# First attention of a fused attention and local-transformer kernel: two buffers for scores and probabilities, a new order of its steps, and the first weight rounding on GpSimd

## What is computed

```python
x = L0_attn_X
xn = _layernorm(x, axis=-1)
x = x + _L0_attn_ref(xn, ...) + _L0_ffn_ref(xn, ...)

def _L0_attn_ref(X, W_q, W_k, W_v, b_q, b_k, b_v):      # one head of width 128
    Q = X @ W_q + b_q; K = X @ W_k + b_k; V = X @ W_v + b_v
    A = softmax(einsum('bsd,btd->bst', Q, K) * scale, axis=2)
    return einsum('bst,btv->bsv', A, V)

def _L0_ffn_ref(x, ...):
    for i in range(6):      # 16 heads of 64, windows of 32 tokens
        x = attn_layer(shift_tokens(x), Wqkv[i], ...) + x
        x = ffn_layer(shift_tokens(x), ...) + x
```

## Time and profile before

| | |
|---|---|
| device time, median of 3 runs | 1501.88 us |
| profiled execution, first to last instruction | 1500.0 us |
| first attention, TensorE's first instruction to the last add | 10.11 to 50.91 us |
| first instruction of the main part on TensorE | 51.27 us |
| TensorE busy, VectorE busy, ScalarE busy, GpSimd busy | 98%, 87%, 85%, 83% |
| mean granted TensorE clock | 0.995 |

### The profile page before, as it was taken

The page is one execution under the profiler, slowest core; times in us unless marked ns, Lnnn a source line. Parts: engine busy times, 40 slices in busy tenths (PEclk is TensorE's granted clock), DMA queues, the critical chain, the costliest instruction groups (busy, mean ns, idle before and its releaser), DMA issues.

```text
span 1500.0 us, 66306 instructions
## 1 busy us (share of the span) xinstructions
PE 1464.2 (98%) x26320; PEld 1280.8 (85%) x26320; DVE 1310.1 (87%) x2365; ACT 1267.7 (85%) x2551; POOL 1248.7 (83%) x1213
## 2 busy tenths in 40 slices
PE   6799999999999999999999999999999999999997
PEld 5578888888888888888888888888888888888886
DVE  6799998889889898888898898889898988998974
ACT  4578888889888888888898888888888888888886
POOL 5489988888888888888888888888888888888781
PEclk9899999999999999999999999999999999999999
DMA  6012212111212111121211121211112121112111
GB/s 185 22 46 60 59 46 57 43 49 42 59 49 79 52 47 43 54 63 52 70 41 50 43 70 49 69 45 50 47 40 55 52 54 38 49 35 52 38 49 39
DMA packets 96184, 80.28 MB, mean 54 GB/s; under 512 B 66282, under 2 KB 79598, under 8 KB 95854
## 3 DMA queue, kind: packets, MB, share of 16 engines
q1 hardware_dynamic: 94990, 75.34, 18.8%
q10 hardware_dynamic: 864, 0.26, 0.1%
HBM read 17.91 MB, written 1.05 MB: 13 GB/s over the span
## 4 chain that ended last, share of the span: by engine, by line
PE 93%; issue 2%; DVE 2%; POOL 1%; ACT 1%; DMA 0%; ACTq 0%; DVEq 0%; POOLq 0%
PE bank L1065 74%; PE bank L1179 11%; PE bank L1217 6%; PE bank L1251 1%; PE bank L1149 1%; DMA rot<-in_b_v 0%; POOL rot L459 0%; DVE parts L891 0%; DVE newton L910 0%; DVE s L937 0%; DVE n L901 0%; DVE am L825 0%; POOL w_lo L446 0%; ACTq L550 0%; ACT rot L576 0%
## 5 line engine op out<-in xcount | busy, mean ns | idle before, releaser
L459 POOL TENSOR_TENSOR rot<-parts 128x512 f32<-128x512 f32 x384 | 493.3, 1285 | 120.4 <-DVE parts L891 120.3
L891 DVE TENSOR_TENSOR parts<-bank,rtab 128x1024 f32<-128x1024 f32 x384 | 459.8, 1208 | 0.4 <-POOL rot L459 0.3
L470 POOL TENSOR_TENSOR rot<-rot,rnorm 128x512 f32<-128x512 f32 x384 | 391.1, 1046 | 10.0 <-DVE rnorm L917 10.0
L901 DVE TENSOR_REDUCE n<-sq 128x8 f32<-128x512 f32 x384 | 257.7, 671 | 33.0 <-ACT sq L627 33.0
L689 ACT ACTIVATE pz<-bank 64x512 f32<-64x512 f32 x384 | 226.1, 589 | 61.4 <-PE bank L1217 59.1
L1065 PE MATMUL bank<-w_hi,x_hi 128*128 128x512 f32 x576 | 263.8, 458 | 4.6 <-DVE parts L891 3.6
L476 POOL TENSOR_TENSOR es<-es,r 128x512 f32<-128x512 f32 x192 | 202.6, 1055 | 75.2 <-DVE r L943 75.2
L627 ACT ACTIVATE sq<-bank 128x512 f32<-128x512 f32 x384 | 230.4, 601 | 28.0 <-DVE n L901 22.0
L1065 PE MATMUL bank<-w_hi,x_lo 128*128 128x512 f32 x576 | 229.5, 398 | 0.0
L1065 PE MATMUL bank<-w_lo,x_hi 128*128 128x512 f32 x576 | 229.1, 398 | 0.0
L1179 PE MATMUL bank<-ident,rot 128*128 128x128 f32 x1536 | 203.1, 275 | 5.0 <-POOL rot L470 2.4
(11 more groups left out here) (86 smaller groups left out, 2660.4 us busy)
## 6 DMA issues: line engine op xcount, KB each, us to landing
vb<-v SPq DMA_DIRECT2D x96, 384.0 KB, 3.8
w_new<-in_Wqkv SPq DMA_DIRECT2D x36, 256.0 KB, 4.2
vb<-v SPq DMA_DIRECT2D x48, 128.0 KB, 3.4
w_o<-in_Wo SPq DMA_DIRECT2D x12, 256.0 KB
xin<-x_tok SPq DMA_DIRECT2D x48, 64.0 KB, 2.1
xs<-x_tok SPq DMA_DIRECT2D x48, 64.0 KB, 2.0
xin<-x_tok SPq DMA_DIRECT2D x48, 56.0 KB, 2.7
xs<-x_tok SPq DMA_DIRECT2D x48, 56.0 KB, 2.0
```

The source lines that it names most:

```text
L459: g.tensor_tensor(rot[:, i * CH:(i + 1) * CH].rearrange(halves, z=2, c=HD), parts[:, b:b + CH].rearrange(halves, z=2, c=HD), parts[:, b + ...
L470: g.tensor_tensor(c, c, over(r, CHH, DH), ALU.mult).then_inc(s_sc[i], 1)
L891: d.tensor_tensor(parts[:, b:b + 2 * CH].rearrange("p (w h c) -> p w h c", w=2, c=DH), heads(bank[QK_BANK[i]][:, :]).unsqueeze(1).to_broad ...
L901: d.tensor_reduce(n2[:, T * 2 * HEADS + m * CHH:T * 2 * HEADS + (m + 1) * CHH], heads(sq[:, b:b + CH]), op=ALU.add, axis=AX.X).then_inc(s_ ...
```

## The change

`pS`, `aprob`, `am2`, `as2` and `ar2` get a second buffer, chosen by s % 2; the second bank for scores is bank 2, which nothing used in this stage. All waits that protected the single buffer look back two sequences instead of one. The order of `first_attention(s)` changes in all three streams, normalising and transposing of x move one sequence earlier, and the loops start at s = -2. The rounding of layer 0's weights goes from ScalarE's stream to GpSimd's, as `tensor_copy` ahead of each subtraction.

```diff
-        aprob = early(TILES * LEN)
+        aprob = early(2 * TILES * LEN)
...
-        pT, pS, pP, pO, pF = bank[3:8]
+        pS = (bank[2], bank[4])
+        pT, pP, pO, pF = bank[3], bank[5], bank[6], bank[7]
...
+        def two(t, s):
+            return t[:, (s % 2) * TILES:(s % 2 + 1) * TILES]
...  GpSimd
+            def split_first(c):
+                pool.wait_ge(s_wq[c], 16)
+                w = slice(c * CH, (c + 1) * CH)
+                g.tensor_copy(w_hi[:, w], w_new[:, w]).then_inc(s_wh, 1)
+                split_lo(0, c)
             for c in range(WCH):
-                split_lo(0, c)
+                split_first(c)
...  ScalarE
             def first_exps(s):
                 act.wait_ge(s_a["neg"], nth(1, s, 1))
-                act.wait_ge(s_a["pt"], nth(1, s - 1, 1))
-                act.wait_ge(s_a["rec"], nth(1, s - 1, 1))
+                act.wait_ge(s_a["pt"], nth(1, s - 2, 1))
+                act.wait_ge(s_a["rec"], nth(1, s - 2, 1))
...
             def first_attention(s):
+                if some(s + 1):
+                    first_bias(s + 1)
+                if some(s + 2):
+                    first_copy_x(s + 2)
                 if some(s - 1):
                     first_copy_p(s - 1)
-                if some(s + 1):
-                    first_copy_x(s + 1)
                 if some(s):
                     first_exps(s)
-                if some(s + 1):
-                    first_bias(s + 1)
...
-            for s in range(-1, SEQS + 1):
+            for s in range(-2, SEQS + 1):
                 first_attention(s)
-                if 0 <= s < WCH:
-                    split_hi(0, s)
...  VectorE
             def first_attention(s):
                 if some(s):
                     first_maxima(s)
-                if some(s + 2):
-                    first_normalise(s + 2)
+                if some(s - 1):
+                    first_add(s - 1)
+                if some(s + 3):
+                    first_normalise(s + 3)
                 if some(s + 1):
                     first_bias(s + 1)
-                if some(s - 1):
-                    first_add(s - 1)
                 if some(s):
                     first_reciprocals(s)
...
-            for s in range(-1, SEQS + 1):
+            for s in range(-2, SEQS + 1):
...  TensorE
             def first_attention(s):
-                if some(s - 1):
-                    first_turn_p(s - 1)
-                if some(s + 1):
-                    first_turn_x(s + 1)
                 if some(s):
                     first_scores(s)
                 if some(s + 1):
                     first_project(s + 1)
+                if some(s + 2):
+                    first_turn_x(s + 2)
                 if some(s - 1):
+                    first_turn_p(s - 1)
                     first_values(s - 1)
-            for s in (-1, 0, 1):
-                first_attention(s)
-            for s in range(2, SEQS + 1):
+            for s in range(-2, SEQS + 1):
                 first_attention(s)
```

More of the change, by code:

```diff
@@ L150, in program @@
         rs0 = sb("rs0", SEQS * TILES)
-        am2 = sb("am2", TILES)
-        as2 = sb("as2", TILES)
-        ar2 = sb("ar2", TILES)
+        am2 = sb("am2", 2 * TILES)
+        as2 = sb("as2", 2 * TILES)
+        ar2 = sb("ar2", 2 * TILES)
         bank = [ctx.enter_context(nc.psum_tensor(f"bank{i}", [P, CH], F32)) for i in range(8)]
         pQ = bank[0:2]
-        pT, pS, pP, pO, pF = bank[3:8]
+        pS = (bank[2], bank[4])
+        pT, pP, pO, pF = bank[3], bank[5], bank[6], bank[7]
         s_first = sem("s_first")
@@ L551, in _ @@
             act.wait_ge(s_first, 16 * NFIRST)
-            a.activation(as2[:, :], ident[:, 0:TILES], ACT.Exp)
+            a.activation(two(as2, 0), ident[:, 0:TILES], ACT.Exp)
             def first_copy_p(s):
@@ L572, in first_exps @@
                 act.wait_ge(s_a["neg"], nth(1, s, 1))
-                act.wait_ge(s_a["pt"], nth(1, s - 1, 1))
-                act.wait_ge(s_a["rec"], nth(1, s - 1, 1))
+                act.wait_ge(s_a["pt"], nth(1, s - 2, 1))
+                act.wait_ge(s_a["rec"], nth(1, s - 2, 1))
                 for T in range(TILES):
-                    a.activation(aprob[:, T * LEN:(T + 1) * LEN], pS[:, T * LEN:(T + 1) * LEN], ACT.Exp,
-                                 scale=float(P) ** -0.5, bias=am2[:, T:T + 1],
-                                 accum_out=as2[:, T:T + 1]).then_inc(s_a["exp"], 1)
+                    o = (s % 2) * TILES * LEN + T * LEN
+                    a.activation(aprob[:, o:o + LEN], pS[s % 2][:, T * LEN:(T + 1) * LEN], ACT.Exp,
+                                 scale=float(P) ** -0.5, bias=two(am2, s)[:, T:T + 1],
+                                 accum_out=two(as2, s)[:, T:T + 1]).then_inc(s_a["exp"], 1)
             def first_attention(s):
+                if some(s + 1):
+                    first_bias(s + 1)
+                if some(s + 2):
+                    first_copy_x(s + 2)
                 if some(s - 1):
                     first_copy_p(s - 1)
-                if some(s + 1):
-                    first_copy_x(s + 1)
                 if some(s):
                     first_exps(s)
-                if some(s + 1):
-                    first_bias(s + 1)
             def split_hi(l, c):
@@ L823, in first_maxima @@
                 dve.wait_ge(s_a["s"], nth(1, s, 1))
-                dve.wait_ge(s_a["exp"], nth(2, s - 1, 2))
-                d.tensor_reduce(am2[:, :], pS[:, :].rearrange("p (t k) -> p t k", t=TILES), op=ALU.max, axis=AX.X)\
-                 .then_inc(s_a["max"], 1)
+                dve.wait_ge(s_a["exp"], nth(2, s - 2, 2))
+                d.tensor_reduce(two(am2, s), pS[s % 2][:, :].rearrange("p (t k) -> p t k", t=TILES), op=ALU.max,
+                                axis=AX.X).then_inc(s_a["max"], 1)
                 dve.wait_ge(s_a["max"], nth(1, s, 1))
-                d.tensor_scalar(am2[:, :], am2[:, :], -float(P) ** -0.5, None, ALU.mult).then_inc(s_a["neg"], 1)
+                d.tensor_scalar(two(am2, s), two(am2, s), -float(P) ** -0.5, None, ALU.mult).then_inc(s_a["neg"], 1)
             def first_bias(s):
@@ L841, in first_add @@
                     o = acc[:, bass.ds(s * LEN + T * P, P)]
-                    last = d.scalar_tensor_tensor(out=o, in0=pO[:, T * P:(T + 1) * P], scalar=ar2[:, T:T + 1],
+                    last = d.scalar_tensor_tensor(out=o, in0=pO[:, T * P:(T + 1) * P], scalar=two(ar2, s)[:, T:T + 1],
                                                   in1=o, op0=ALU.mult, op1=ALU.add)
@@ L847, in first_reciprocals @@
                 dve.wait_ge(s_a["exp"], nth(2, s, 2))
-                dve.wait_ge(s_a["done"], nth(1, s - 1, 1))
-                d.reciprocal(ar2[:, :], as2[:, :]).then_inc(s_a["rec"], 1)
+                dve.wait_ge(s_a["done"], nth(1, s - 2, 1))
+                d.reciprocal(two(ar2, s), two(as2, s)).then_inc(s_a["rec"], 1)
             def first_attention(s):
@@ L867, in _ @@
             dve.wait_ge(s_first, 16 * NFIRST)
-            for s in range(-1, SEQS + 1):
+            for s in range(-2, SEQS + 1):
                 for i in range(1, len(PARTS)):
-                    if s + 2 == PARTS[i][0]:
+                    if s + 3 == PARTS[i][0]:
                         dve.wait_ge(s_l0p, i + 1)
@@ L1074, in first_turn_p @@
                         last = t.transpose(pP[:, (k * TILES + T) * P:(k * TILES + T + 1) * P],
-                                           aprob[:, T * LEN + k * P:T * LEN + (k + 1) * P], ident[:, :])
+                                           aprob[:, (s % 2 * TILES + T) * LEN + k * P:(s % 2 * TILES + T) * LEN + (k + 1) * P],
+                                           ident[:, :])
                 last.then_inc(s_a["pt"], 1)
@@ L1087, in first_scores @@
                 pe.wait_ge(s_a["k"], nth(1, s, 1))
-                pe.wait_ge(s_a["exp"], nth(2, s - 1, 2))
+                pe.wait_ge(s_a["exp"], nth(2, s - 2, 2))
                 for T in range(TILES):
-                    last = mm(pS[:, T * LEN:(T + 1) * LEN], aq[:, T * P:(T + 1) * P], ak[:, :])
+                    last = mm(pS[s % 2][:, T * LEN:(T + 1) * LEN], aq[:, T * P:(T + 1) * P], ak[:, :])
                 last.then_inc(s_a["s"], 1)
```

## The result

The changed kernel takes 1509.32 us (median of 4 runs, 1508.74 to 1510.81) against 1501.68 for the kernel before beside it (4 runs, 1501.24 to 1501.92). The ratio is 1.0054, with a 95% interval of 1.0040 to 1.0067: slower by 7.6 us. The forecast was 1512.0.

What follows compares the result with a forecast made beforehand. TensorE bounds the kernel, so the last add of the first attention sets the time: start 19.9, rings to project(7) at 51.05, tail 10.2, so 61.2 against 50.91; +10.1 after correction, 1512.0 us. Own range 1508 to 1515, 8-in-10 range 1506.5 to 1519.

Steps and rivals of the forecast that it cites:

- What sets the time: At the hand-over to the main part on TensorE: the first attention's last add decides, 61.2 against 50.91 us.
- The ring: Closed loop of waits between TensorE, ScalarE and VectorE in first attention: 5.75 us a sequence, against 4.19 before.
- Its two waits: TensorE's uncovered waits in each loop: 0.7 us for the copy of p, 1.2 us for v's bias.
- The signs: Trace signs in first attention: TensorE waits for v's bias before project and the copy of p before values, seven times each.
- The second buffers at nothing: In first attention, the waits that second buffers remove do not end last in the new order: costed at nothing.
- The rival in which they free TensorE: Second buffers let TensorE run first attention at its own work, 3.67 us a sequence: 1499.5 us, chance 0.04.
- GpSimd's hold: Busy GpSimd delays VectorE's normalise until 35.6 us: 1.5 us more for each of two sequences.
- The start and the tail: Both ends of first attention: project(2) at 19.9 us, and 10.2 us from project(7) to the last add.
- the correction that I had taken off: The same working gave the old order's last add 51.1 where the trace has 50.91, so 0.2 us came off.
- The clock: Rival: TensorE's clock falls in first attention because it is busy only 64% of each loop; 1520 to 1531 us, chance 0.10.

Runs made afterwards that it cites:

- e1: Changed kernel with VectorE's add(s-1) moved behind normalise(s+3) and bias(s+1); 1503.86 us, 1.0012 of the kernel before.
- e7: Changed kernel with VectorE's normalise(s+3) moved ahead of add(s-1), bias still behind the add; 1506.72 us, 1.0027 of the kernel before.
- e2: Changed kernel with TensorE's transposes of p right behind the scores and ScalarE's copy of p ahead of the biases; 1502.43 us, 1.0002 of the kernel before.
- e3: Changed kernel with both the edits of e1 and e2; 1499.26 us, 0.9981 of the kernel before.
- e9: Changed kernel with GpSimd's layer 0 rounding and subtraction held until after the last add; only the stage is read, 48.16 us.
- e10: e5 with GpSimd's layer 0 rounding and subtraction held until after the last add; only the stage is read, 48.75 us.
- e11: e8 with one buffer for scores, probabilities and sums, waits looking back one sequence; 1503.30 us, 1.0003 of the kernel before.
- e8: Changed kernel with e2's TensorE and ScalarE order, add last on VectorE, layer 0 rounding back on ScalarE; 1497.55 us, 0.9965 of the kernel before.
- e6: Changed kernel with layer 0's rounding back on ScalarE behind each sequence; 1510.35 us, 1.0051 of the kernel before.
- e5: Changed kernel with one buffer for scores, probabilities, maxima, sums and reciprocals, waits looking back one sequence; 1510.80 us, 1.0052 of the kernel before.
- e4: Kernel before with only layer 0's rounding moved from ScalarE to GpSimd, order and buffers unchanged; 1502.26 us, 1.0000 of the kernel before.
- e12: e8 with layer 0's rounding on GpSimd, as in the change; 1499.27 us, 0.9979 of the kernel before.

## Why the prediction was right, step by step

- **What sets the time.** The hand-over to the main part follows the last add by 0.36 us before and 0.35 after, and the main part kept its length within what it varies anyway; over its first 49 us the mean granted clock was 0.86 in both traces. The end of the stage was the right place to look.
- **The ring.** Forecast 5.75 us, measured 5.75 twice (project at 32.25, 38.00 and 43.75), and 5.24 without normalise (forecast 5.15). Its two waits were forecast as 0.7 and 1.2 and read 0.69 and 0.84 on the products, 0.93 and 1.21 on the weight loads. That the sum agrees to the hundredth is partly luck, since turn_p up to the copy was priced 0.07 too low, project and turn_x 0.04 too low, and add, normalise and bias 0.10 too high. e1 took the add out of the ring, e7 the normalise, and e2 the copy of p, while it also let the add start sooner; they gave 6.1, 3.5 and 7.8 us back. The two waits are not additive: either edit shortens the one ring, so 6.1 and 7.8 together are more than the 10.2 that e3 gave back. The signs were there less evenly than forecast: TensorE waits for v's bias ahead of six projects and for the copy of p ahead of eight values, where the forecast had seven each.
- **The second buffers at nothing.** Right for the ring (e9 against e10, both 5.75). For the first sequence the 0.58 us between them are not told apart from the slow first loads. The rival in which they free TensorE failed here and is real in another order (e11 against e8).
- **GpSimd's hold.** This is the term that was mis-sized. The mechanism is the one forecast: e9 removes it, e6 moves it onto all four rings that have a normalise, e7 hides it. I took 1.5 us for each of two rings; they were 6.70 and 6.25, so 0.95 and 0.50, 1.55 less in all. The 1.5 came from normalising beside the table and a first subtraction. The copy was 0.61 us where I took 1.0, and the last subtraction ended at 33.07, not 35.6. In each of the two rings one of the two normalising instructions met a copy, and only the other had to sit out the rest of a subtraction. How much of the 1.55 is the shorter copy and how much the moment at which the instructions met is not shown; e5, with the same copy, had 7.05 twice, 1.30 of hold in each ring. The expectations for e4 and e12 were too high in the same way.
- **The start and the tail.** From TensorE's first instruction to project(2) 9.99 us (forecast 9.79); from project(7) to the last add 10.10 (10.2). The stage grew by 8.98 against 10.1 forecast: 1.55 less from the hold, 0.2 more at the start, 0.2 for the correction that I had taken off, and 0.0 from the rest.
- **The clock.** The granted clock stayed at 1.00, 2.4 GHz, over the later rings with 8.45 of 11.52 us busy (the row below), and also over the two rings beside GpSimd, with 4.23 of 6.70 and 4.23 of 6.25. So that rival did not come about. The forecast had set its 64%, which counts weight loads, beside the 57% of the earlier trace rows, which counts products; by products the ring is 73% busy, so the rival was argued on unlike figures:

```profile
37.47:48.99 11.52, 8.45 (x52) 6.92 (x52) 4.58 (x18) 5.59 (x16) 0.00 (x0) 1.00 0.08 17
```

The profiled execution came out 2.8 us under its forecast of 1510.1. Of these 1.1 are the stage; the rest is the earlier first instruction, 0.8, and the shorter main part, 0.9, which vary by as much from trace to trace. That more than half of the miss is of this kind is chance, and says nothing for or against the working.

## What to carry to other kernels

A second buffer is worth only what its wait costs in the order that it stands in: here nothing in a ring of one order and 0.83 us a period (4.55 against 3.72) in another. Before an order of steps is changed, write down for each wait what the waiting engine has queued behind it and who waits for that; a step that waits for the very last product of an iteration must not stand ahead of one that the next iteration's first products need. Between a producer on TensorE and its consumer on the same engine, put other products that are as long as the copy in between.

## What the runs showed of the hardware that I had not expected

- A GpSimd copy of 128x512 from fp32 to fp32r takes 0.61 us, half of the 1.27 of a subtraction of that size, and close to a memset's 0.53.
- VectorE's tensor-scalar and cast instructions that meet a GpSimd instruction under way end when that one ends: two normalising instructions take 0.59 to 0.60 us beside an idle GpSimd, and 1.09 us (the changed kernel) to 2.44 (e8) where they meet its instructions. Its additions from PSUM, reductions and reciprocals stay at 0.41, 0.67 and 0.15. What the hold costs depends on when instructions meet: from the first transposes of p to the last add e9, with neither, takes 36.81 us; subtractions alone, started by ScalarE (e6), add 2.7, and the full work of GpSimd (the changed kernel) only 1.45.
- TensorE's first eight weight loads take 2.63 us and the eight of a later project 1.38, and the granted clock reads 1.00 over both. How long the slow stretch lasts varies: the next twelve loads take 2.26 us (e4) to 3.65 (e5). Between e4 and the kernel before, and between e12 and e8, whose steps on TensorE are the same, this is 0.94 of the 0.95 and 0.65 of the 0.66 us by which the start up to the first transposes of p differs. What sets its length was not tried.
